# Normalising tokens on ScalarE instead of VectorE in the project stage of a transformer block

## The reference

```python
h = _layernorm(x, axis=-1) * (1 + ca) + sa          # (x - m) / sqrt(v + eps)
q = h @ W_q
latent_kv = (h @ W_k + h @ W_v) @ W_down_kv
k_rec = latent_kv @ W_up_k                          # then heads of 16
v_rec = latent_kv @ W_up_v
scores = einsum('bhqd,bhkd->bhqk', q, k_rec) / sqrt(256) * decay
```

## Time and profile before

| | us |
|---|---|
| median of 3 runs | 2543.09 |
| the runs | 2543.0 to 2543.3 |
| the profiled execution | 2542.97 |
| its span | 2541.2 |
| project stage, first split to the barrier behind it | 38.0 to 347.1 |

### The profile page before, as it was taken

The page is one execution under the profiler, slowest core; times in us unless marked ns, Lnnn a source line. Parts: engine busy times, 40 slices in busy tenths (PEclk is TensorE's granted clock), DMA queues, the critical chain, the costliest instruction groups (busy, mean ns, idle before and its releaser), DMA issues. The chain is left out here.

```text
span 2541.2 us, 41434 instructions
## 1 busy us (share of the span) xinstructions
PE 2378.6 (94%) x12682; PEld 1051.1 (41%) x12682; DVE 2075.1 (82%) x3811; ACT 1841.7 (72%) x4193; POOL 1330.2 (52%) x1110
## 2 busy tenths in 40 slices
PE   5887858999999999999999999999987999999998
PEld 2433312333333333333333333333323666666665
DVE  5888878888888888888888888888866888888885
ACT  3666614888888888888888888888883555555554
POOL 3666651543543534535435435345234788888884
PEclk9677756999999999999999999999997999999999
DMA  4777894575674665656745746547413222222210
GB/s 139 250 247 248 249 224 118 129 146 116 136 153 101 149 139 113 156 120 127 153 111 137 151 101 156 132 113 153 98 43 97 62 66 68 67 59 67 66 45 19
DMA packets 274797, 319.28 MB, mean 126 GB/s; under 512 B 38152, under 2 KB 182280, under 8 KB 274448
## 3 DMA queue, kind: packets, MB, share of 16 engines
q1 hardware_dynamic: 265360, 308.24, 49.6%
q10 hardware_dynamic: 9216, 8.39, 0.9%
HBM read 229.45 MB, written 85.49 MB: 124 GB/s over the span
## 5 line engine op out<-in xcount | busy, mean ns | idle before, releaser
L943 DVE CUSTOM_DVE_ANT_0 unread<-max_ps,toeplitz_sb 128x1024 bf16<-128x1024 f32 x1024 | 1215.7, 1222 | 248.6 <-PE max_ps L760 246.3
L872 ACT ACTIVATE probs<-score_ps 128x512 f32<-128x512 f32 (+3 forms) x2560 | 1015.1, 483 | 149.9 <-PE score_ps L789 75.5
L760 PE MATMUL max_ps<-k_low,q_low 96*128 96x512 bf16 x2048 | 717.8, 392 | 27.6 <-DVE ident_bf L934 17.9
L715 POOL TENSOR_TENSOR diag<-diag,diag_decay 128x512 f32<-128x512 f32 x240 | 305.7, 1274 | 811.0 <-ACT diag L881 806.1
L815 PE MATMUL pv_ps<-probs,v 128*32 128x512 f32 x4096 | 545.3, 605 | 1.7 <-ACT probs L901 0.7
L784 PE MATMUL score_ps<-q_up,k_up 99*128 99x512 bf16 (+3 forms) x1280 | 407.6, 319 | 13.9 <-ACT probs L872 12.4
L789 PE MATMUL score_ps<-q_low,k_low 99*128 99x512 bf16 (+3 forms) x1280 | 403.3, 317 | 3.6 <-ACT probs L872 3.0
L727 POOL TENSOR_TENSOR diag<-diag,shift 128x512 f32<-128x512 f32 x256 | 333.8, 1304 | 81.9 <-DVE diag L967 62.4
L1384 PE MATMUL gu_ps<-wgu_t,turned 128*128 128x512 f32 (+1 forms) x768 | 317.1, 563 | 0.8 <-DVE hid L1606 0.8
L760 PEld LDWEIGHTS max_ps<-k_low,q_low 96*128 96x128 bf16 x2048 | 197.0, 98 | 217.8 <-DVE row_max L943 107.7
L784 PEld LDWEIGHTS score_ps<-q_up,k_up 99*128 99x128 bf16 x1280 | 123.5, 97 | 378.2 <-ACT probs L872 200.5
(11 more groups left out here) (157 smaller groups left out, 2839.1 us busy)
## 6 DMA issues: line engine op xcount, KB each, us to landing
shift<-max_whole_dram SPq DMA_DIRECT2D x64, 1024.0 KB, 7.9
splits<-parts SPq DMA_DIRECT2D x128, 384.0 KB, 2.7
q_low<-splits SPq DMA_DIRECT2D x192, 128.0 KB, 7.1
k_low<-splits SPq DMA_DIRECT2D x192, 128.0 KB, 8.1
q_up<-splits SPq DMA_DIRECT2D x192, 128.0 KB, 10.8
k_up<-splits SPq DMA_DIRECT2D x192, 128.0 KB, 11.8
v_padded<-v_out SPq DMA_DIRECT2D x64, 256.0 KB, 3.7
v<-v_padded SPq DMA_DIRECT2D x32, 512.0 KB, 13.8
```

The lines of the kernel that those rows point to most:

```text
L715: nc.gpsimd.tensor_tensor(diag[:, g % 2], diag[:, g % 2], diag_decay[:].unsqueeze(1).broadcast_to([P, UH, P]), ALU.mult).then_inc(diag_dec ...
L760: mm = pe.matmul(max_ps[:, i % 2, half * HALF:(half + 1) * HALF], low[0][u][0:KROWS, h, qb * P:(qb + 1) * P], low[1][u][0:KROWS, h, half * ...
L872: op = nc.scalar.activation(probs[:, g % PROBS, h, first:end], score_ps[:, at % RING, first:end], ACT.Exp)
L943: nc.vector.tensor_tensor_reduce(unread[:, i % 2, :], max_ps[:, i % 2, :], toeplitz[:, at:at + S], 1.0, -3.0e38, ALU.mult, ALU.max, row_ma ...
```

## The change

ScalarE makes `xhat` as rstd * x + offset, where offset is -mean * rstd. VectorE makes -mean beside var_eps, GpSimd the product behind the power. ScalarE normalises half h + 2 at n = 6 of half h; VectorE's normalise is gone. The load of x for half h + 3 is issued between the second and third store of half h, and waits for `xhat` of half h + 1 instead of `x_free`; three halves are loaded ahead at the start. `POOL_RESTS` is empty, so every branch on it leaves all subtractions `rest` where they are.

```diff
         def load_x(b, hf):
             h = 2 * b + hf
-            sp.wait_ge(x_free, h + 1)
+            if h >= 2:
+                sp.wait_ge(xhat_ready, TH * (h - 1))
...
             for n in range(BLOCKS):
                 nb = BLOCKS * (2 * b + hf) + n
                 tensor, chunk, version = n // 4, n // 2 % 2, n % 2
+                if n == 2 and later(b, hf, 3):
+                    load_x(*later(b, hf, 3))
                 sp.wait_ge(low_ready, nb + 1)
...
             for hf in range(2):
-                if later(b, hf, 2):
-                    load_x(*later(b, hf, 2))
                 store(b, hf)
 
         load_x(0, 0)
         load_x(0, 1)
+        load_x(1, 0)
...
             dve.wait_ge(stats_done, count)
+            if h > 0:
+                dve.wait_ge(rstd_ready, h)
...
             nc.vector.tensor_scalar(var_eps[:], mean_var[:, :, 1], EPS, None, ALU.add).then_inc(var_ready, 1)
-
-        def normalise(b, hf):
-            h = 2 * b + hf
-            dve.wait_ge(rstd_ready, h + 1)
-
-            for i in range(TH):
-                op = nc.vector.tensor_scalar(xhat[hf][:, i, :], x_in[hf][:, i, :], mean_var[:, i, 0:1],
-                                             rstd[:, i:i + 1], ALU.subtract, ALU.mult)
-                op.then_inc(xhat_ready, 1)
-            dve.wait_ge(xhat_ready, TH * (h + 1))
-            dve.sem_inc(x_free, 1)
+            nc.vector.tensor_scalar(minus_mean[:], mean_var[:, :, 0], -1.0, None, ALU.mult).then_inc(var_ready, 1)
...
         def steps(b):
             for hf in range(2):
-                if later(b, hf, 1):
-                    normalise(*later(b, hf, 1))
                 splits(b, hf)
 
         statistics(0, 0)
-        normalise(0, 0)
         statistics(0, 1)
...
         def inverse_std(h):
-            pool.wait_ge(var_ready, h + 1)
-            nc.gpsimd.tensor_tensor(rstd[:], var_eps[:], minus_half[:], ALU.pow).then_inc(rstd_ready, 1)
+            pool.wait_ge(var_ready, 2 * (h + 1))
+            if h > 0:
+                pool.wait_ge(xhat_ready, TH * h)
+            nc.gpsimd.tensor_tensor(rstd[:], var_eps[:], minus_half[:], ALU.pow).then_inc(inverse_ready, 1)
+            pool.wait_ge(inverse_ready, h + 1)
+            nc.gpsimd.tensor_tensor(offset[:], minus_mean[:], rstd[:], ALU.mult).then_inc(rstd_ready, 1)
...
+        def normalise(b, hf):
+            h = 2 * b + hf
+            act.wait_ge(rstd_ready, h + 1)
+            for i in range(TH):
+                nc.scalar.activation(xhat[hf][:, i, :], x_in[hf][:, i, :], ACT.Identity, bias=offset[:, i:i + 1],
+                                     scale=rstd[:, i:i + 1]).then_inc(xhat_ready, 1)
...
         def steps(b):
             for hf in range(2):
                 for n in range(BLOCKS + 1):
+                    if n == 6 and later(b, hf, 2):
+                        normalise(*later(b, hf, 2))
...
+        normalise(0, 0)
         modulate(0, 0)
+        normalise(0, 1)
```

More of the change, by code:

```diff
@@ L162, in project_stage @@
     RING = 8
+    POOL_RESTS = ()
     def sb(name, shape, dt):
@@ L176, in project_stage @@
     rstd = sb("rstd", [P, TH], F32)
+    minus_mean = sb("minus_mean", [P, TH], F32)
+    offset = sb("offset", [P, TH], F32)
     h_t = [sb(f"h_t{i}", [P, DC, HALF], F32) for i in range(2)]
@@ L199, in project_stage @@
         sem("full_ready"), sem("high_ready"), sem("rest_ready"), sem("middle_ready"), sem("low_ready"))
-    x_free, lat_free, q_free, k_free = sem("x_free"), sem("lat_free"), sem("q_free"), sem("k_free")
+    lat_free, q_free, k_free = sem("lat_free"), sem("q_free"), sem("k_free")
+    inverse_ready, pool_rest_ready = sem("inverse_ready"), sem("pool_rest_ready")
     parts_free = [sem(f"parts_free{i}") for i in range(RING)]
@@ L259, in _ @@
     def _(dve):
-        dve.sem_inc(x_free, 2)
         dve.sem_inc(q_free, 1)
@@ L295, in scaled @@
                 source = (q_ps, k_ps)[tensor]
+                if n in POOL_RESTS and h > 0:
+                    dve.wait_ge(pool_rest_ready, len(POOL_RESTS) * (h - 1) + POOL_RESTS.index(n) + 1)
                 dve.wait_ge((q_ready, k_ready)[tensor], DC * h + chunk + 1)
@@ L311, in splits @@
                     scaled(n)
-                if n > 0:
+                if n > 0 and n - 1 not in POOL_RESTS:
                     without_high(n - 1)
@@ L346, in low_parts @@
                 nb = BLOCKS * (2 * b + hf) + n
-                pool.wait_ge(rest_ready, nb + 1)
+                if n in POOL_RESTS:
+                    pool.wait_ge(high_ready, nb + 1)
+                    nc.gpsimd.tensor_tensor(rest[:, n % RING, :], full[:, n % RING, :], parts[:, n % RING, 0, :],
+                                            ALU.subtract).then_inc(pool_rest_ready, 1)
                 pool.wait_ge(middle_ready, nb + 1)
@@ L462, in middle @@
         def middle(b, hf, n):
-            act.wait_ge(rest_ready, BLOCKS * (2 * b + hf) + n + 1)
+            h = 2 * b + hf
+            if n in POOL_RESTS:
+                act.wait_ge(pool_rest_ready, len(POOL_RESTS) * h + POOL_RESTS.index(n) + 1)
+            else:
+                others = [i for i in range(BLOCKS) if i not in POOL_RESTS]
+                act.wait_ge(rest_ready, len(others) * h + others.index(n) + 1)
             nc.scalar.activation(parts[:, n % RING, 1, :], rest[:, n % RING, :], ACT.Copy).then_inc(middle_ready, 1)
```

## The result

The changed kernel takes 2524.35 us in the median (2521.91 to 2525.72), the kernel before beside it 2543.2: ratio 0.9917, interval 0.9906 to 0.9929, 21 us faster by the ratio. The forecast was 2512, range 2494 to 2528. The profiled execution took 2521.91 (span 2520.0).

The account below looks back on a forecast made before the run. Bound: each half's loop, where VectorE normalises at the end while ScalarE waits. 14 halves x 2.5 us, less 1.1 at the start and 2.7 at the end, is 31.2 us off 2543.1: about 2512, range 2494 to 2528.

Parts of the forecast that it names:

- VectorE's `xhat` at a half's end, all on the path: End of each half: removing VectorE's four normalise instructions takes 3.05 us off the path.
- ScalarE's activations, 0.5 us a step and 2.0 a half: Four added normalise activations before the sixth high: 2.0 us a half, bounds 1.6 and 2.5; two waits behind can shrink.
- `offset` at 1.0 us, just hidden: GpSimd's product behind the power takes 1.0 us, ready at t = 10.5, before ScalarE arrives at 10.75.
- The latent copy (t = 1.93) and the anchor at t = 9.05 don't move: In a half, the latent copy and ScalarE's second copy of v keep their times, t = 1.93 and 9.05.
- Half 7 as the model of all: The half starting at 171.80, laid out step by step: 16.3 us for 18.50, a saving of 2.2 us.
- The granted clock "should if anything rise": TensorE's two gaps shrink to about one of 1 us, pulling the second copy of v forward: 0.3 us a half.
- B: Rival, chance 0.16: TensorE's clock stays up and ScalarE's wait at the second copy of v shrinks; 3.5 us a half, 2498.
- The load of x, 0.2 us a half: Issuing x earlier removes VectorE's wait before the statistics, of which only 0.17 us reached ScalarE: 0.2 us a half.
- Rests and low parts "one after another": VectorE's rests and GpSimd's low parts exclude each other, about 12.8 us a half, below 16.3: delays but doesn't bound.
- C: Rival, chance 0.22: ScalarE's work simply adds, through collisions after every normalise or `offset` late by 0.7; 1.5 us a half, 2526.
- D: Rival, chance 0.05: the wait only moves, `k_ps`, `rest` or TensorE's lower clock holding halves at 18.8; 2543, no change.
- E: Rival, chance 0.05: ScalarE waits for late stores to free slots of `parts`; halves of 19.2 us, 2548.5, slower.

Follow-up runs that it names:

- e3: Changed kernel without ScalarE's normalise of halves 2 to 15, which only waits for rstd and signals: 2505.69 us, ratio 0.9856.
- e7: Changed kernel with GpSimd's low parts made for 128 of 512 columns only, zeros instead of the rest: 2494.36 us, ratio 0.9820.
- e4: Changed kernel with the queue's loads of toeplitz and the twelve others spread over halves 4 to 10 instead of one burst: 2516.21 us, ratio 0.9896.
- e1: Kernel before with only the load of x moved a half earlier, VectorE still normalising: 2537.23 us, ratio 0.9983.
- e2: Changed kernel with x loaded at the start of a half's stores, two halves ahead, as before: 2556.45 us, ratio 1.0052.
- e8: e4 plus two filler matmuls in TensorE's gap and the normalise split two and two tiles into ScalarE's waits: 2495.29 us, ratio 0.9825.
- e5: e4 plus two f32 filler matmuls of 128x512 on TensorE before its wait for the latent's copy: 2511.23 us, ratio 0.9886.

## Why the prediction was right, and where it was off

Direction and range held; the gain was put at 31 us and is 19 by the medians, 21 by the ratio, and 23 at the stage's end in the profiled execution.

*VectorE's `xhat` at a half's end, all on the path:* right. The wait of 3.18 us is gone. The 54.1 us of the earlier trace rows, though, are not this wait alone, as the prediction reads them, but all waits of a high for `full`; those before first splits are 45.9 us in halves 0 to 13. The sum didn't use them.

*ScalarE's activations, 0.5 us a step and 2.0 a half:* right, 585 ns each and 2.06 for four. That their cost on the path would be under 2.0, since the two waits behind them shrink, was in the layout, and e3 measured it at 1.1 to 1.5.

*`offset` at 1.0 us, just hidden:* it takes 0.20, and ScalarE never waits for it. That it fitted was partly luck. In the short half at 142.06 the power started at t = 9.25, not 8.5, since GpSimd's fourth low part ended only at 9.07 and `var_eps` with it; `offset` was ready at 10.54, where 10.5 was forecast, and ScalarE came at 10.93. In the long half of the changed kernel GpSimd's line is:

```profile
168.15 1.01 POOL L340 TENSOR_TENSOR rstd<-var_eps,minus_half 128x4 f32<-128x4 f32 x1 [0.25 <-DVE minus_mean L285]
169.24 0.20 POOL L342 TENSOR_TENSOR offset<-minus_mean,rstd 128x4 f32<-128x4 f32 x1
```

*"The latent copy (t = 1.93) and the anchor at t = 9.05 don't move":* this step failed. I had GpSimd's last low part run to 17.4, 1.1 us into the next half, and used that for the queue at half 14 but not for VectorE's first `rest`, which then meets it (the second of GpSimd's two low parts here ends at 177.84):

```profile
175.11 2.73 POOL L352 TENSOR_TENSOR parts<-rest,parts 128x512 bf16<-128x512 f32 x2
176.99 1.40 DVE L305 TENSOR_TENSOR rest<-full,parts 128x512 f32<-128x512 f32 x1
```

In the kernel before, the 3 us of `xhat` had kept the two apart: that `rest` took 0.69 us in every half. The delay of 0.70 us goes through the latent's copy into k, v and the second copy of v. e7 shows it: without the long low part the copy is back at 1.92.

*Half 7 as the model of all:* half 7 was the kernel before at its second copy of v by 9.05. In nine of halves 0 to 13 that copy was at 9.78, with the clock low through k and v. 9.78 + 0.70 is 10.48, which the long halves show. The 16.3 of the layout is met by the short ones (16.46), but by luck: there the delay of 0.70, a second copy of v that the upper clock brings to 8.2 or a little later, and a `full` 5 held up by `var_eps` come to high 5 at 9.80, for the 9.65 of the layout. So 2.5 us a half became 2.00, and 14 x 0.5 is the 7 us that the stage's end lacks to the forecast, with another 0.9 from the end: I took 2.7 given back there, and it was 3.3 in half 14 and 0.2 in half 15. e4 shows that these hang on the burst in the queue.

*The granted clock "should if anything rise", for 0.3 us a half:* it rose from 0.73 to 0.76, too little to pull the copy of v forward in six of the fourteen halves. In the other eight it did come forward, and the held-up `full` 5 took that gain away. I put TensorE's gaps at one of 1 us; it is 2.9, since a faster TensorE only waits longer for a later latent copy, the argument I had held against B.

*The load of x, 0.2 us a half:* right for the kernel before by luck (e1 gives 3.4 us at the stage's end), since the 0.17 us before high 5 that it was read from is ScalarE's wait for its own copies and stays in e1 and in the changed kernel's long halves; the gain came from other halves than half 7. It is wrong as a price in the changed kernel (e2), where the load decides the sign of the whole. The prediction priced each part against the kernel before; this part had to be priced against the kernel with the others in. I had seen that ScalarE would run ahead of GpSimd and the queue, and had not asked what else stands in that queue.

*Rests and low parts "one after another", 8 x 1.6 = 12.8 us:* by the shortest times of the earlier trace rows a pair is 0.67 + 1.15 = 1.82 us and eight are 14.6. That is under 16.3, so the conclusion holds, but there is much less room than the prediction says, and collisions are to be expected; it laid out one, and in a short half three reach ScalarE.

*Rivals.* C's time was the nearest (2526), but its mechanism is true only in part: `offset` isn't late, and the collision behind the normalise (a wait of 0.78 us) was in the forecast's layout; what the layout lacked is the one at the start of a half and, in short halves, the one at `var_eps`. B is what e8 produces on purpose (a granted clock of 0.93 over halves 1 to 12); e5 comes near it with 0.83. D and E didn't happen; the wait on a slot of `parts` within halves 0 to 13 is nowhere in the changed kernel.

## What to carry to other kernels

When a stall at the end of a loop goes, look at who used it to catch up: here GpSimd's last subtraction, the DMA queue and the load at its end all slide into the next round, and one of them alone (the load) would have turned a gain of 0.8% into a loss of 0.5%. Moved work is cheapest in the receiving engine's waits; the same four activations cost 1.1 to 1.5 us in one piece and 0.3 in two. Lay out more than one period, one for each kind that the trace shows, and look at the tiny instructions too: what they wait for is in their duration.

## What the runs showed of the hardware

- A subtraction of 128x512 on VectorE with two SBUF inputs took 674 ns alone and up to 1.64 us beside GpSimd's subtractions; with these cut to 128 columns its mean fell from 917 to 689 ns. The recorded duration holds the wait: a tensor_scalar of 128x4 takes 0.16 or 0.17 us, or 0.90 to 1.13 when GpSimd's low part started first, and it ends with it (151.16 and 151.13 in the short half above). The Trainium skill, "SBUF — State Buffer", section "Who interferes with whom", says that the one that issues second is blocked until the first has finished; the trace agrees.
- TensorE went between its two levels from one half to the next at the same work (1.98 and 3.78 us for the same four matmuls, at a granted clock of 1.00 and 0.50); two idle-time matmuls a half brought the granted clock from 0.73 to 0.83 over halves 1 to 12. The Trainium skill, "TensorE: Matmul & The Clock Gate", section "HAM oscillation — how this bites in real kernels", ties such changes to idle gaps, in a kernel whose gaps are longer than the 2.9 us here; that filling one helps agrees with it, that some halves stay at the lower level with it filled isn't explained by any run here.
- An f32 activation of 128x256 in SBUF with two column operands takes 585 ns, 0.49 us from start to start.
